# Two subtractions on GpSimd and a new order of steps in a two-layer transformer kernel

## What is computed

```python
x = L0_attn_x                                          # (32, 256, 128)
x = _layernorm(x + _L0_attn_ref(x, ...), axis=-1)      # stages A: 16 heads of 8, ALiBi bias, softmax
x = _layernorm(x + _L0_ffn_ref(x, ...), axis=-1)       # stages B: 8 experts, top 2, and a shared one
x = _layernorm(x + _L1_attn_ref(x, ...), axis=-1)      # stages C: keys and values at 16 fixed shifts, gated
x = _layernorm(x + _L1_ffn_ref(x, ...), axis=-1)       # stages D: 8 linear experts, top 2
return x
```

## Time and profile before

| | us |
|---|---|
| median of 3 runs (1558.98 to 1560.1) | 1559.63 |
| the profiled execution | 1561.28 |
| its span, first to last instruction | 1559.5 |
| busy PE, DVE (share of the span) | 1392.1 (89%), 1319.1 (85%) |
| busy ACT, POOL | 843.3 (54%), 660.3 (42%) |
| mean granted TensorE clock | 0.970 |

### The profile page before, as it was taken

One profiled execution on the slowest core, in us unless ns is written; L12 is line 12 of the kernel. 1 busy time (PEld: TensorE's weight loads), 2 busy tenths in 40 slices (PEclk: granted clock), 3 DMA queues, 4 the chain that ended last, 5 costly groups with the idle time before them and its releaser, 6 DMA issues.

```text
span 1559.5 us, 34559 instructions
## 1 busy us (share of the span) xinstructions
PE 1392.1 (89%) x11872; PEld 1081.4 (69%) x11872; DVE 1319.1 (85%) x4159; ACT 843.3 (54%) x1806; POOL 660.3 (42%) x484
## 2 busy tenths in 40 slices
PE   4899899999999999999999999999999999997632
PEld 2677677777777777777777777777777777765521
DVE  4677899888899988888889898888898988867765
ACT  1666555566666555666665555666655556553310
POOL 0013355544443455434434555344345554444442
PEclk9999999999999999999999999999999999988866
DMA  5412234444332344343323443433234444231222
GB/s 150 132 63 62 82 99 112 113 106 109 96 83 78 94 113 112 106 112 93 87 80 86 113 113 106 113 102 84 80 89 104 113 110 105 69 71 43 56 60 44
DMA packets 77931, 145.90 MB, mean 94 GB/s; under 512 B 8747, under 2 KB 64299, under 8 KB 64683
## 3 DMA queue, kind: packets, MB, share of 16 engines
q1 hardware_dynamic: 77758, 143.70, 34.6%
HBM read 118.24 MB, written 25.17 MB: 92 GB/s over the span
## 4 chain that ended last, share of the span: by engine, by line
DVE 39%; PE 38%; issue 10%; DMA 4%; ACT 4%; POOL 1%; DVEq 0%; ACTq 0%; POOLq 0%; SPq 0%
DVE prod L917 8%; PE bPV L495 7%; DVE nBy L974 7%; PE bTU L479 6%; DVE mneg L1021 5%; DVE h L1031 5%; DVE nDy L955 5%; PE bS L538 4%; DMA prod<-d_w 3%; PE bTU L481 3%; PE bTU L550 2%; PE b L419 2%; PE bTU L551 2%; PE bS L541 2%; PE b L436 2%
## 5 line engine op out<-in xcount | busy, mean ns | idle before, releaser
L1085 POOL TENSOR_TENSOR prod<-prod 128x1024 f32<-128x1024 f32 (+2 forms) x160 | 290.0, 1813 | 205.7 <-DVE prod L917 198.1
L1093 POOL TENSOR_TENSOR prod<-kC,qC 128x512 f32<-128x512 f32 x256 | 322.3, 1295 | 125.7 <-ACT kC L672 125.7
L1021 DVE TENSOR_REDUCE mneg<-bS 128x2 bf16<-128x512 f32 x512 | 346.5, 693 | 32.8 <-PE bS L541 32.7
L708 ACT ACTIVATE sil<-bTU,b 128x256 f32<-128x256 f32 x288 | 136.7, 475 | 306.0 <-PE bTU L551 302.9
L698 ACT ACTIVATE P<-bTU 128x512 f32<-128x512 f32 x512 | 279.3, 603 | 11.8 <-PE bTU L481 11.4
L538 PE MATMUL bS<-stack 96*128 96x256 bf16 x1024 | 222.7, 279 | 52.3 <-DVE mneg L1021 46.1
L479 PE MATMUL bTU<-stack 97*128 97x256 bf16 x1024 | 209.8, 276 | 0.4 <-DMA stack<-mT 0.2
L541 PE MATMUL bS<-dist,identh 128*128 128x128 f16 x1024 | 198.9, 222 | 0.0
L917 DVE TENSOR_TENSOR prod<-prod,vC 128x512 f32<-128x512 f32 x256 | 185.0, 776 | 15.1 <-DMA prod<-d_w 15.1
L481 PE MATMUL bTU<-dist,identh 128*128 128x128 f16 x1024 | 192.0, 221 | 0.0
L550 PE MATMUL bTU<-x1T,w 128*128 128x256 f32 x576 | 175.9, 387 | 6.0 <-DVE h L1031 6.0
(11 more groups left out here) (155 smaller groups left out, 2422.9 us busy)
## 6 DMA issues: line engine op xcount, KB each, us to landing
prod<-d_w SPq DMA_DIRECT2D x64, 1024.0 KB, 9.7
stack<-d_parts SPq DMA_DIRECT2D x192, 192.0 KB
d_parts<-parts SPq DMA_DIRECT2D x96, 128.0 KB, 6.9
d_w<-wT SPq DMA_DIRECT2D x32, 256.0 KB, 2.1
xT<-in_xT SPq DMA_DIRECT2D x32, 128.0 KB, 10.2
x<-in_x SPq DMA_DIRECT2D x32, 128.0 KB, 2.3
out_x<-xout SPq DMA_DIRECT2D x32, 128.0 KB, 2.1
stack<-in_rows SPq DMA_DIRECT2D x6, 192.0 KB
```

Of the source, the lines that this page charges most:

```text
L1021: v.tensor_reduce(mneg[:, :, k], bS[k % 2][:].rearrange("p (a b) -> p a b", a=TT), op=ALU.max, axis=AX.X, negate=True).then_inc(dveS.done( ...
L1085: tt_(pv[e % 2][:, to:to + rows_, :], pv[e % 2][:, to:to + rows_, :], pv[e % 2][:, frm:frm + rows_, :], ALU.add).then_inc(poolSum.done("ad ...
L1093: tt_(prod[e % 2][:, 2 * p:2 * p + 2, :], shifted(kC, p), qC[:].unsqueeze(1).to_broadcast([128, 2, T]), ALU.mult).then_inc(poolC1.done("pr ...
```

## The change

A1.rest and A1.lo are issued by POOL instead of DVE, as the same two subtractions; they signal a semaphore of their own (poolA1), and DVE's now counts A1.v alone. POOL's wait for the constants moves from its start to pass 2. The lists of all five engines are in a new order.

```diff
--- before.py
+++ after.py
@@ -47,26 +47,27 @@
 
 ORDER = {
     "pe": """
-        A1.qk A1.v S.s.0 S.s.1 A2.ST.0 A2.ST.1 A2.ST.2 S.s.2 A2.ST.3 A2.ST.4 Cs.scT A2.ST.5 S.s.3 A2.ST.6 A2.PV.0
-        B.xT A2.ST.7 A2.ST.8 A2.ST.9 D.xT S.s.4 S.s.5 B.lg D.lg A2.ST.10 A2.ST.11 Cs.wT A2.PV.1 C1.xT S.s.6 A2.ST.12
-        C1.qk A2.ST.13 A2.ST.14 A2.PV.2 A2.ST.15 B.cT S.s.7 D.y.0 B.ab.0 D.y.1 S.s.8 S.s.9 A2.PV.3 S.s.10 B.ab.1
-        B.ab.2 C1.vg S.s.11 B.ab.3 S.s.12 S.s.13 A3.pT B.ab.4 D.y.2 B.ab.5 S.s.14 C1.sc A3.aT D.y.3 B.ab.6 S.s.15
-        B.y.0 A3.out B.ab.7 B.ab.8 B.y.1 B.y.2 M.mT B.y.3 B.z C2.out""",
+        A1.qk A1.v S.s.0 S.s.1 A2.ST.0 A2.ST.1 A2.ST.2 S.s.2 Cs.scT A2.ST.3 A2.ST.4 A2.ST.5 A2.ST.6 A2.PV.0 A2.ST.7
+        A2.ST.8 S.s.3 A2.PV.1 B.xT A2.ST.9 S.s.4 D.xT Cs.wT A2.ST.10 S.s.5 B.lg D.lg C1.xT A2.ST.11 A2.ST.12 C1.qk
+        S.s.6 S.s.7 D.y.0 A2.PV.2 B.cT A2.ST.13 S.s.8 A2.ST.14 S.s.9 A2.ST.15 S.s.10 D.y.1 D.y.2 C1.vg B.ab.0 S.s.11
+        S.s.12 B.ab.1 A2.PV.3 S.s.13 B.ab.2 B.ab.3 A3.pT B.ab.4 B.y.0 S.s.14 C1.sc S.s.15 A3.aT B.ab.5 B.ab.6 B.y.1
+        A3.out B.ab.7 B.ab.8 M.mT B.y.2 D.y.3 B.y.3 B.z C2.out""",
     "act": """
-        A1.qk A2.exp.0 A2.exp.1 A2.exp.2 A2.exp.3 A2.exp.4 A2.exp.5 A3n.nm A2.exp.6 C2n.nm B.xT Cs.exp D.xT A2.exp.7
-        A2.exp.8 B2.nm A2.exp.9 A1.mid Cs.wT A2.exp.10 C1.xT G.ge A2.exp.11 A2.exp.12 C1.qk A2.exp.13 A2.exp.14 B.cT
-        A2.exp.15 D2.nm B.ab.0 B.ab.1 A3.cp B.ab.2 C1.vg B.ab.3 B.ab.4 B.ab.5 A3.aT C1.sc B.ab.6 B.ab.7 B.ab.8 M.mT""",
+        A1.qk A2.exp.0 A2.exp.1 A2.exp.2 A2.exp.3 A2.exp.4 Cs.exp A2.exp.5 A2.exp.6 A2.exp.7 A1.mid A3n.nm C2n.nm
+        B.xT B2.nm D.xT A2.exp.8 Cs.wT A2.exp.9 C1.xT A2.exp.10 G.ge A2.exp.11 C1.qk A2.exp.12 D2.nm A2.exp.13 B.cT
+        A2.exp.14 A2.exp.15 B.ab.0 B.ab.1 C1.vg A3.cp B.ab.2 B.ab.3 B.ab.4 B.ab.5 B.ab.6 A3.aT C1.sc B.ab.7 B.ab.8
+        M.mT""",
     "dve": """
-        B2.res D2.mom A1.rest S.max.0 N.root.0 A1.v N.root.1 S.max.1 N.root.2 N.root.3 Cs.mx S.max.2 S.max.3 Cs.sum
-        S.max.4 G.rank S.max.5 G.weigh A1.lo S.max.6 D.acc.0 S.max.7 S.max.8 D.acc.1 B.wu.0 S.max.9 S.max.10 C2.pv.0
-        B.wu.1 S.max.11 B.wu.2 C2.pv.1 C2.pv.2 C2.pv.3 B.wu.3 S.max.12 A3.rec B.wu.4 D.acc.2 A3.num C2.pv.4 C2.pv.5
-        C2.pv.6 C2.pv.7 S.max.13 B.wu.5 D.acc.3 B.wu.6 S.max.14 B.acc.0 S.max.15 B.wu.7 A3.res B.wu.8 B.acc.1
-        B.acc.2 C2.gt B.acc.3 C2.res""",
+        A1.v S.max.0 B2.res D2.mom Cs.mx N.root.0 N.root.1 S.max.1 N.root.2 S.max.2 N.root.3 Cs.sum S.max.3 S.max.4
+        S.max.5 G.rank G.weigh S.max.6 S.max.7 D.acc.0 S.max.8 S.max.9 D.acc.1 S.max.10 D.acc.2 S.max.11 C2.pv.0
+        S.max.12 B.wu.0 B.wu.1 C2.pv.1 C2.pv.2 C2.pv.3 B.wu.2 B.wu.3 A3.rec S.max.13 A3.num B.wu.4 B.acc.0 C2.pv.4
+        C2.pv.5 C2.pv.6 C2.pv.7 S.max.14 B.wu.5 S.max.15 B.wu.6 B.acc.1 A3.res B.wu.7 B.wu.8 B.acc.2 D.acc.3 C2.gt
+        B.acc.3 C2.res""",
     "pool": """
-        A3.xbo C2.xb C1.prod.0 C1.prod.1 C1.prod.2 C1.prod.3 C1.prod.4 C1.prod.5 C1.prod.6 C1.prod.7 C2.add.0
-        C2.add.1 C2.add.2 C2.add.3 C2.add.4""",
+        A1.rest C2.xb A1.lo C1.prod.0 C1.prod.1 C1.prod.2 C1.prod.3 C1.prod.4 C1.prod.5 C1.prod.6 C1.prod.7 C2.add.0
+        A3.xbo C2.add.1 C2.add.2 C2.add.3 C2.add.4""",
     "sp": """
-        A3.x Cs.dw A1.part.0 Cs.wb A1.part.1 C2.wb X.xT A1.part.2 A1.rows.0 A1.rows.1 A1.rows.2 M.m D2.out""",
+        Cs.dw Cs.wb C2.wb A3.x A1.part.0 X.xT A1.part.1 A1.part.2 A1.rows.0 A1.rows.1 A1.rows.2 M.m D2.out""",
 }
 ORDER = {engine: [(".".join(step.split(".")[:2]), int((step.split(".") + [0])[2])) for step in order.split()]
          for engine, order in ORDER.items()}
@@ -222,7 +223,7 @@
         actCs = steps("actCs", "exp wT")
         actD = steps("actD", "xT")
         actG = steps("actG", "ge")
-        dveA1, dveS = steps("dveA1", "rest v lo"), steps("dveS", "max*16")
+        dveA1, poolA1, dveS = steps("dveA1", "v"), steps("poolA1", "rest lo"), steps("dveS", "max*16")
         dveA3 = steps("dveA3", "rec num*2 " + LN)
         dveG = steps("dveG", GATE)
         dveB, dveY = steps("dveB", "wu*9"), steps("dveY", "acc*16")
@@ -320,7 +321,7 @@
                         elif n == 1:
                             sp.wait_ge(actMid.sem, actMid.count(e, "mid"))
                         else:
-                            sp.wait_ge(dveA1.sem, dveA1.count(e, "lo"))
+                            sp.wait_ge(poolA1.sem, poolA1.count(e, "lo"))
                         sp.dma_start(d_parts[:, n].rearrange("s p n -> p s n"), parts[:, :, n, :]).then_inc(st_part[n], 16)
                     if what == "A1.rows" and (e := r["A1"]) is not None:
 
@@ -643,7 +644,7 @@
                 for what, n in ORDER["act"]:
                     if what == "A1.qk" and (e := r["A1"]) is not None:
                         act.wait_ge(peA1.sem, peA1.count(e, "qk"))
-                        act.wait_ge(dveA1.sem, dveA1.count(e - 1, "lo"))
+                        act.wait_ge(poolA1.sem, poolA1.count(e - 1, "lo"))
                         act_f(qk[:, 0, :], b6[:, 0:T], ACT.Identity, bias=bqk0[:, 0:1],
                               scale=qs0[:, 0:1]).then_inc(actA1.done("q"), 1)
                         act_f(qk[:, 1, :], b6[:, T:2 * T], ACT.Identity, bias=bqk0[:, 1:2]).then_inc(actA1.done("k"), 1)
@@ -655,7 +656,7 @@
                               bias=bqk0[:, 1:2]).then_inc(actA1.done("hi", 1), 1)
                     if what == "A1.mid" and (e := r["A1"]) is not None:
                         act.wait_ge(st_part[1], dma_count(e - 1))
-                        act.wait_ge(dveA1.sem, dveA1.count(e, "rest"))
+                        act.wait_ge(poolA1.sem, poolA1.count(e, "rest"))
                         nc.scalar.copy(parts[:, :, 1, :], rest[:]).then_inc(actMid.done("mid"), 1)
                     if what == "B.xT" and (e := r["B"]) is not None:
                         act.wait_ge(peB.sem, peB.count(e, "xT"))
@@ -891,10 +892,6 @@
                 rows = slice(present[0], present[-1] + 1) if present else None
                 eN = t - LAG["A3n"]
                 for what, n in ORDER["dve"]:
-                    if what == "A1.rest" and (e := r["A1"]) is not None:
-
-                        dve.wait_ge(actA1.sem, actA1.count(e, "hi", 1))
-                        v.tensor_tensor(rest[:], qk[:], parts[:, :, 0, :], ALU.subtract).then_inc(dveA1.done("rest"), 1)
                     if what == "A1.v" and (e := r["A1"]) is not None:
                         dve.wait_ge(peA1.sem, peA1.count(e, "v"))
                         dve.wait_ge(pePV.sem, pePV.count(e - 3, "PV", 3))
@@ -902,11 +899,6 @@
                         v.tensor_tensor(o, b7[:, 0:T].rearrange("p (a r d) -> p a r d", r=2, d=HD),
                                         bv0[:].rearrange("p t c -> p (t c)").rearrange("p (a r d) -> p a r d", r=2, d=HD),
                                         ALU.add).then_inc(dveA1.done("v"), 1)
-                    if what == "A1.lo" and (e := r["A1"]) is not None:
-                        dve.wait_ge(st_part[2], dma_count(e - 1))
-                        dve.wait_ge(actMid.sem, actMid.count(e, "mid"))
-                        v.tensor_tensor(parts[:, :, 2, :], rest[:], parts[:, :, 1, :],
-                                        ALU.subtract).then_inc(dveA1.done("lo"), 1)
                     if what == "C2.pv" and (e := r["C2"]) is not None:
 
                         p = n
@@ -1063,13 +1055,21 @@
         @block.gpsimd
         def _(pool):
             tt_ = nc.gpsimd.tensor_tensor
-            pool.wait_ge(ld_const, 16 * N_CONST)
 
             def one(t):
                 r = stages(t)
+                if t == LAG["A3"]:
+                    pool.wait_ge(ld_const, 16 * N_CONST)
                 if t == LAG["C1"]:
                     pool.wait_ge(setup_dve, SETUP_DVE)
                 for what, n in ORDER["pool"]:
+                    if what == "A1.rest" and (e := r["A1"]) is not None:
+                        pool.wait_ge(actA1.sem, actA1.count(e, "hi", 1))
+                        tt_(rest[:], qk[:], parts[:, :, 0, :], ALU.subtract).then_inc(poolA1.done("rest"), 1)
+                    if what == "A1.lo" and (e := r["A1"]) is not None:
+                        pool.wait_ge(st_part[2], dma_count(e - 1))
+                        pool.wait_ge(actMid.sem, actMid.count(e, "mid"))
+                        tt_(parts[:, :, 2, :], rest[:], parts[:, :, 1, :], ALU.subtract).then_inc(poolA1.done("lo"), 1)
                     if what == "A3.xbo":
                         if (e := r["A3"]) is not None:
                             pool.wait_ge(ld_x, dma_count(e))
```

## The result

The changed kernel takes 1542.55 us (median of 4 runs, 1540.46 to 1545.89) against 1559.31 us for the kernel before in the same comparison: a ratio of 0.9894 with a 95% interval of 0.9882 to 0.9905. It is faster, by 16.8 us or 1.1%, a little under half of the 36 us forecast (1523), and inside the range. One run of a later experiment, e11_pv0_two_earlier, took 2743.97 us where its three others took 1526.72 to 1532.46; it is left out.

The account below looks back on a forecast made before the run. A loop through PE, ACT and DVE was taken to set the 44.28 us pass. At 43.1 us, 27 x 1.2 = 32 us, plus 5 in the last passes, less 1 in pass 0, gave 36: 1523 us, range 1502 to 1551.

Parts of the forecast that it names:

- step 4: DVE from S.max.11's end to L1002: no gap, 17.6 us of work, loop closes at 42.8 us.
- PE's own work: One of three close loops: PE's C2.out ready at 43.3 us, where L1002 at 43.0 asks for 43.56.
- Step 1: PE and ACT, pass start: exp.0 still at 5.21 us, S.s.2 doesn't wait, ST.3 waits about 1.0 us.
- Step 2: ACT from exp.0 on, exponentials, norms and copy of x1T: D.xT can start on PE at 12.13 us.
- Step 3: PE from D.xT: no wait, 12.55 us of work, S.s.11 starts at 24.7, its maximum at 25.2.
- (d): Slower rival: first C2.pv products on DVE meet C1.prod on POOL; pass up to 46.2 us, time 1607; chance 0.12.
- Step 5: POOL: C2.pv.7 ends at 35.9 us, last four adds take 6.94, so L1002 can't start before 43.0.
- Step 6: Old loop through ACT's D2.nm: closes at 41.3 us, no longer the bound; 2.93 us wait shrinks to some tenths.
- The subtractions: A1.rest and A1.lo off DVE: about 1.2 us less work a pass; moved alone, at most 0.1 us saved.
- DMA: SP's reordered loads and stores cost nothing; if the cover goes, C2.pv.0 waits.
- Pass 0 and the end: POOL's slower subtractions lose 1 us in pass 0; covering DVE's Cs.exp wait in the last passes gains 5.
- (b): Less-gain rival: DVE's waits for PE add 0.6 us to the loop; pass 43.7 us, time 1540; chance 0.13.

Follow-up runs that it names:

- e11_pv0_two_earlier: The changed kernel with C2.pv.0 moved ahead of S.max.11 on DVE; 1530.26 us (median of three runs), ratio 0.9801 to the kernel before.
- e3: The changed kernel with C2.pv.0 moved behind B.wu.0 on DVE, two steps later; 1527.21 us, ratio 0.9783 to the kernel before.
- e6: e3 with two exchanges on PE, so that B.xT does not wait 0.30 us for its input; 1524.25 us, ratio 0.9777 to the kernel before.
- e5: The changed kernel with ACT's D2.nm put two exponentials later, behind A2.exp.14; 1644.8 us, ratio 1.0549 to the kernel before.
- e7: e1 with POOL's copy A3.xbo moved from beside n_i to behind C2.add.0; 1561.73 us, ratio 1.0016 to the kernel before.
- e1: The kernel before with only the two subtractions moved to POOL; 1566.27 us, ratio 1.0035 to the kernel before.
- e8: The changed kernel with both subtractions left on DVE and C2.pv.0 moved behind B.wu.0; 1534.55 us, ratio 0.9838 to the kernel before.
- e4: The changed kernel with SP's list of the kernel before; 1541.67 us, ratio 0.9873 to the kernel before.
- e10: Same order as the changed kernel in everything, since its intended edit was already there; 1540.27 us, ratio 0.9876 to the kernel before.

## Why the prediction was right or wrong

The direction, the place of the gain and most of the walk were right; the size was wrong. Of the 0.79 us a pass between 43.1 and 43.89, 0.50 is the clash of C2.pv.0 with a product on POOL, a term of step 4 that was mis-sized, and 0.29 is PE's own work, sized too short.

- **Step 1** held: ST.3 starts at 5.86 us of the pass, 0.83 of waiting for 1.0.
- **Step 2**: D.xT at 12.28 for 12.13. B.xT waits 0.30 for its input, which I had left out of PE's time.
- **Step 3**: S.s.11 at 24.86 for 24.7, S.max.11 at 25.40 for 25.2.
- **Step 4 is the one that failed**, in "taking off ... leaves 17.6. The loop closes at 42.8". The 17.6 carried C2.pv.0 at the 0.98 us, start to start, that it had before. It now takes 1.67 (910.38 to 912.05), 0.69 more, and 0.20 is a wait ahead of B.acc.2. Without these two the stretch is 18.49 - 0.69 - 0.20 = 17.60 us, as reckoned. 25.40 + 17.60 + 0.89 = 43.89. I had named the mechanism under rival (d), with "Now pv.0 alone meets them", and priced there pv.1 to pv.3, which did stay free; pv.0 itself, on a stretch that I had just called gap-free, I left at its old price. The trace of before holds the warning: C2.pv.0 took 1.06 there, above its line's median of 0.69, since it met prod.6 (its end at 912.56):

```profile
912.05 1.06 DVE L917 TENSOR_TENSOR prod<-prod,vC 128x512 f32<-128x512 f32 x1
```

  Where it arrives within the products decides whether it is 0.07 or 1.07 us longer than the median (e3, the change), and my times were not good to 0.1 us. It should have gone in with bounds of 0 to 1.1 us more.
- **Step 5**: the last adds end at 43.8 instead of 42.9. They follow C2.pv.7, which is late by 0.8 us through C2.pv.0; L994 follows them by 0.11 us, as step 5 says, but this is an effect. In e3 the adds end 0.3 us ahead of L994's need.
- **PE's own work** was sized too short. From S.s.11 to C2.out I had 18.6 us; without any wait (e3) it is 19.1. That is why e3 stops at 43.39 and not at 43.1; with the 0.30 wait filled (e6) it is 43.15. The prediction gives no parts for the 18.6, so which of them was short stays open. The forecast pass of 43.1 is thus reached by moving two things that the change did not.
- **Step 6** held (0.29 us left of 2.93), and e5 shows what it carries: with D2.nm late the pass is 3.9 us longer, the lower clock that follows the wait included.
- **The subtractions** were to "save at most the 0.1 us" if moved alone: wrong by sign, 0.4% slower, through n_i beside A3.xbo (e7) and more waits of C2.pv.0 for its DMA (e1). The price of each on POOL was right (1.16 for 1.2, also with the bfloat16 output). I had looked for harm among DVE's large steps with two SBUF inputs and had G.rank only "beside the end of A1.lo". In the changed kernel the neighbourhood has moved: N.root.0 starts at 6.8 us, behind A1.rest's end at 5.1, and n_i is back at 172 ns, ggt at 425. There the move does what I said, it frees DVE and cuts 0.26 us a pass (e8 to e3), because n_b comes 0.6 us and the first norm 0.3 us earlier than with A1.rest on DVE, and PE's wait ahead of B.xT is 0.30 instead of 0.58.
- **DMA** costing nothing held (e4); in the 25 passes of the changed kernel C2.pv.0 never waits for its weights.
- **Pass 0 and the end.** I had 1 us of loss at the start; the profiled execution shows 4.7. The rest is the granted clock, which was at its lower level, 1.2 GHz, in two stretches of the start-up, 10.2 us together. The same order in e10 had it for 3.4 us only and starts up in 178.4. The changed kernel, then e10, in the same two stretches:

```profile
64.30:71.10 6.80, 6.52 (x29) 5.18 (x30) 3.13 (x11) 2.24 (x6) 1.07 (x1) 0.50 0.09 28
108.60:112.00 3.40, 3.40 (x28) 1.86 (x28) 0.32 (x2) 1.69 (x4) 0.00 (x0) 0.50 0.00 0
```

```profile
64.30:71.10 6.80, 6.60 (x50) 4.91 (x50) 4.50 (x17) 4.34 (x10) 1.16 (x1) 0.81 0.21 59
108.60:112.00 3.40, 3.10 (x39) 2.35 (x40) 1.63 (x3) 2.81 (x8) 0.39 (x1) 1.00 0.13 39
```

  At half the clock 10.2 us cost at most 5.1, and 3.4 at most 1.7 (an estimate): 177.0 and 176.7 without them. e3, at the full clock throughout its start-up, has 176.6, and the kernel before, also at the full clock, 177.4. So the new order loses nothing at the start. What decides whether the clock falls there no run here shows. e10's profiled execution is 19.4 us shorter than that of before (span 1540.1), against the 1 - 32 - 5 = -36 of the forecast.

Of the rivals, (d) happened in a small form, and the 1540 of (b) was nearly the time, for another reason: DVE does wait for PE ahead of D.acc.1 and G.rank, but those waits were already in my walk and added nothing. That the time fell near the price of (b) is luck.

The Trainium skill, "SBUF — State Buffer", section "Who interferes with whom", says that of VectorE and GpSimd the one that issues first gets the ports they share for the whole instruction and the other blocks fully, and that issue order decides which. Every pair above agrees: 1.75 us when 0.10 behind prod.7, 0.78 when 0.19 ahead of it, 1.38 when it meets prod.6 half-way. It counts `tensor_scalar` among the operations that can take both ports, when their operands meet its conditions; n_v and n_i, with one input each, agree with 0.48 and 0.65 us instead of 0.16 and 0.17. I had cited the rule for two inputs only.
